# Splitting the row loads' semaphore and fetching the first lone chunk's weights earlier, in a decoder layer on one Trainium2 core

## The reference

```python
x = layernorm(x + mixer(x))            # rmsnorm, causal depthwise conv, min-GRU, GELU feed-forward
x = layernorm(x + cross_attention(x, ctx))   # 16 heads of 64, causal mask
x = layernorm(x + moe(x))
# moe: 16 experts, top 2 of sigmoid(x @ gate_w + gate_b), weights normalised
hg = einsum('bsd,edi->bsei', x, experts_wg); hu = einsum('bsd,edi->bsei', x, experts_wu)
all_outputs = einsum('bsei,eid->bsed', silu(hg) * hu, experts_wd)
return x + shared_mlp(x) + sum(expert_values * selected(all_outputs))
```

## Time and profile before

| | |
|---|---|
| time, median of 3 runs | 1636.52 us (1636.0 to 1638.09) |
| the profiled execution's own time | 1619.51 us |
| its span | 1617.8 us |
| mean granted TensorE clock | 0.938 |
| busy: PE, PEld, DVE, ACT, POOL | 83%, 68%, 59%, 59%, 52% |

### The profile page before, as it was taken

How to read it: one execution, slowest core, us unless ns; L and a number is a source line. 1 busy time by engine, 2 the same in 40 slices (tenths; PEclk the granted TensorE clock), 3 DMA queues, 4 the chain that set the end, 5 groups by cost and what they waited for, 6 DMA issues and landing times. The chain is left out here.

```text
span 1617.8 us, 34460 instructions
## 1 busy us (share of the span) xinstructions
PE 1348.5 (83%) x11280; PEld 1098.5 (68%) x11280; DVE 956.1 (59%) x2616; ACT 946.5 (59%) x3395; POOL 834.8 (52%) x988
## 2 busy tenths in 40 slices
PE   2889897999898988899898998989988998967542
PEld 1667676777786777678776777767776777756442
DVE  3456565565655666566764777556665776555324
ACT  3666656576756666466755667565665766555111
POOL 4343525543555457554556546654566646547244
PEclk9999998999998999889998999989999999989777
DMA  6000000032212312222212212132122212135563
GB/s 207 8 7 8 7 7 15 26 93 59 60 38 83 96 30 67 63 79 78 64 43 69 81 55 71 42 99 79 37 60 82 82 57 61 37 94 154 157 181 84
DMA packets 149425, 109.99 MB, mean 68 GB/s; under 512 B 12736, under 2 KB 144384, under 8 KB 149248
## 3 DMA queue, kind: packets, MB, share of 16 engines
q1 hardware_dynamic: 139328, 89.43, 19.0%
q0 software_dynamic: 8192, 16.79, 3.6%
q10 hardware_dynamic: 1728, 1.57, 0.3%
HBM read 73.14 MB, written 34.60 MB: 67 GB/s over the span
## 5 line engine op out<-in xcount | busy, mean ns | idle before, releaser
L1791 POOL TENSOR_TENSOR pr<-pr,ri 128x480 f32<-128x480 f32 x256 | 251.1, 995 | 303.4 <-DVE ri L1394 299.9
L1068 ACT ACTIVATE pr<-sE,nm 128x120 f32<-128x120 f32 x512 | 178.1, 360 | 240.3 <-DVE nm L1389 222.3
L1056 ACT ACTIVATE pT<-t 120x512 f32<-120x512 f32 x256 | 142.3, 614 | 78.7 <-PE t L528 72.8
L1068 ACT ACTIVATE pr<-sO,nm 128x120 f32<-128x120 f32 x512 | 179.2, 381 | 0.0
L669 PEld LDWEIGHTS sE<-kT,qT 64*128 64x128 f32 x1024 | 131.1, 197 | 55.3 <-issue 55.3
L711 PE MATMUL pvb<-wo,hT 128*128 128x128 f32 x1024 | 137.4, 290 | 31.7 <-DVE hT L1404 31.7
L669 PE MATMUL sO<-kT,qT 64*128 64x120 f32 x1024 | 156.7, 295 | 7.0 <-issue 7.0
L1404 DVE TENSOR_TENSOR hT<-pvb,col 128x512 f32<-128x512 f32 x128 | 87.9, 686 | 126.0 <-PE pvb L702 111.4
L711 PEld LDWEIGHTS pvb<-wo,hT 128*128 128x128 f32 x1024 | 125.8, 200 | 45.5 <-DVE hT L1404 45.0
L669 PE MATMUL sE<-kT,qT 64*128 64x120 f32 x1024 | 155.7, 295 | 0.5 <-issue 0.5
L1820 POOL DMA_INDIRECT sorted_x<-x,slot x128 | 129.8, 1014 | 47.3 <-issue 34.3
(11 more groups left out here) (382 smaller groups left out, 3525.7 us busy)
## 6 DMA issues: line engine op xcount, KB each, us to landing
wq<-in_w_e SPq DMA_DIRECT2D x232, 128.0 KB
sorted_y<-yq SPq DMA_DIRECT2D x68, 256.0 KB
xq<-sorted_x SPq DMA_DIRECT2D x58, 256.0 KB
xt<-in_x SPq DMA_DIRECT2D x16, 256.0 KB, 2.9
sorted_x<-yq SPq DMA_DIRECT2D x16, 256.0 KB, 4.2
cT<-in_ctxT SPq DMA_DIRECT2D x16, 240.0 KB, 3.0
out_y<-y SPq DMA_DIRECT2D x48, 64.0 KB
sorted_x<-x,slot POOLq DMA_INDIRECT x128
```

The lines of the kernel that those rows point to most:

```text
L1056: f(pT[:, 4 * r:4 * r + 4, :], seqs((t0, t1)[r][0:S, :]), ACT.Copy).then_inc(sem[f"probsT{r}_sb"], 1)
L1068: ins = f(pr[:, p % RING, r, i, :], score_banks[r][:, i * S:(i + 1) * S], ACT.Exp, bias=nm[:, p % 2, r, i:i + 1], accum_out=rsum[:, p % 2, ...
L1791: GP.tensor_tensor(pr[:, p % RING, r, :, :], pr[:, p % RING, r, :, :], ri[:, p % 2, r, :, :].to_broadcast([P, 4, S]), ALU.mult).then_inc(s ...
```

## The change

The row loads of chunk 7 signal two semaphores: quads 56 to 59 the first, 60 and 61 the second. One semaphore is given up for it in POOL's prologue. In SP's order the weights of 56 and 57 are loaded in halves of two tiles in slots 4 to 7, and the waits for the buffers move to slot 4. Slot 8 then loads rows 56 to 59 and the weights of 58, in front of its output store; slot 9 the weights of 59; slot 10 those of 60 with a wait for `d_down(54)`. Behind the step only the weights of 61 are left, and `d_store(56)` follows them.

```diff
-ONCE = [..., "mask0", "mask", ..., *[f"xq_last{i}" for i in range(3)], ...]
+ONCE = [..., "mask", ..., *[f"xq_last{i}" for i in range(4)], ...]
 def x_last_in(n):
-    return ("xq_last0", LONE_QUADS) if i < LONE_QUADS else (f"xq_last{1 + (i - LONE_QUADS) // 3}", 3)
+    return ("xq_last0", 4) if i < 4 else ("xq_last1", 2) if i < LONE_QUADS else (f"xq_last{2 + (i - LONE_QUADS) // 3}", 3)
...
-            def w_load(n):
+            def w_load(n, lo=0, hi=QUAD):
...
-                for u in range(QUAD):
+                for u in range(lo, hi):
...
                             d_store(n + s - 3)
+                        if s == 4:
+                            for name in ("a_bank", "ln1_out"):
+                                sp.wait_ge(sem[name], whole(name, G - 1))
+                        if 4 <= s < 8:
+                            w_load(LAST + (s - 4) // 2, s % 2 * 2, s % 2 * 2 + 2)
+                        if s == 8:
+                            for i in range(4):
+                                x_load(LAST + i)
+                        if s == 10:
+                            sp.wait_ge(sem["d_down"], upto("d_down", 0, LAST - 2))
+                        if s >= 8:
+                            w_load(LAST + s - 6)
                         for e, q in sums_in(es, s - 1):
                             e_store(e, q)
-                        if s == 8:
-                            for name in ("a_bank", "ln1_out"):
-                                sp.wait_ge(sem[name], whole(name, G - 1))
-                            for i in range(4):
-                                x_load(LAST + i)
-                        if s >= 8:
-                            w_load(LAST + s - 8)
...
                 x_load(LAST + 4 + i)
-            w_load(LAST + 3)
             sp.wait_ge(sem["d_down"], upto("d_down", 0, LAST - 1))
-            w_load(LAST + 4)
+            w_load(LAST + 5)
             d_store(LAST)
-            w_load(LAST + 5)
             d_store(LAST + 1)
...
-            GP.memset(maskb[:], 0.0).then_inc(sem["mask0"], 1)
+            GP.memset(maskb[:], 0.0).then_inc(sem["ones"], 1)
...
-            pool.wait_ge(sem["mask0"], 1)
+            pool.wait_ge(sem["ones"], 2)
...
-            pool.wait_ge(sem["ones"], 2)
+            pool.wait_ge(sem["ones"], 3)
```

More of the change, by code:

```diff
@@ L123 @@
 LATE_LOADS = ["wk", "wv", "wq", "ff2", "wo", "wrs", "wsd"]
-ONCE = ["waits_held", "mixer_weights", *[f"{n}_in" for n in LATE_LOADS], "w_hi", "w_lo", "ident", "identb", "mask0", "mask", "iota", "iotaf", "ones", "gammas", "bq8", "powers", "pads",
+ONCE = ["waits_held", "mixer_weights", *[f"{n}_in" for n in LATE_LOADS], "w_hi", "w_lo", "ident", "identb", "mask", "iota", "iotaf", "ones", "gammas", "bq8", "powers", "pads",
         "tri", "onesb", "zeros", "xs_zeroed",
-        *[f"xq_last{i}" for i in range(3)], *[f"wq_last{i}" for i in range(4)]]
+        *[f"xq_last{i}" for i in range(4)], *[f"wq_last{i}" for i in range(4)]]
 A_USE = {n: k for k, n in enumerate(
```

## The result

The changed kernel takes 1623.53 us (median of 22 runs, 1612.49 to 1635.32). The kernel before took 1633.23 us in the same comparison (22 runs, 1623.93 to 1638.09). The ratio is 0.9944 with an interval of 0.9925 to 0.9963: a gain of 9.1 us by the ratio, 6.0 to 12.2 by its interval. The forecast was a gain of 14.0 us and a time of 1622.5.

What follows compares the result with a forecast made beforehand. PE was taken as the bound for most of the span, SP's issue order at the chunk's end; 12.2 + 2.4 - 0.6 = 14.0 us off 1636.52 gives 1622.5, range 1620 to 1625, or 1617 to 1628 with rivals (a) and (b).

Steps and rivals of the forecast that it cites:

- the first term: PE's wait for `xq` before the transposes of quad 56 goes, since two semaphores split the row loads: 12.2 us gained.
- The inputs that I named as next: After the hole, attention sum, normalised output and weights of 56 to 58 all come before 1509, at most a tenth late.
- The step that the weights of 58 must come in time: In SP's changed order the weights of 58 land by 1505.4, before `d_up(56)` wants them at 1508.6.
- The second term: Weights two quads ahead remove PE's stall at `d_up(59)` for quad 61's weights: 2.4 us, bounds 1.3 and 2.4.
- rival (a): Only the stall before quad 56 goes; SP loses its lead, quad 61's weights come late again: gain 9 to 12, chance 0.13.
- Expected sign: If the forecast is right, `d_up(59)` runs without a DMA wait, where before it stood 2.44 us.
- The price of the halves: Half a quad in slots 4 to 7 costs SP 2.2 us each, hidden in its idle time; 0.6 us for late landings.
- The sign that I had named as wrong: `d_up(52)` to `d_up(55)` waiting longer for `wq`, or a new wait for `hf` or `keep_sb` at `d_up(56)`.
- rival (c): SP becomes the bound of slots 4 to 7 and stretches each; 3.0 us slower net, time 1639.5, chance 0.03.
- Rival (b), the clock: Without the hole PE's clock stays up, work from 1518.05 to 1522.5 takes 2.6 not 4.4 us: gain 16, chance 0.10.
- move with the quads and do not absorb a gain: PE's later gaps, 7.03 us up to 1546.54 and 7.32 us up to 1570.15, are chained to what goes before them.
- A sign of being right: PE's distance from `d_T(56)` to the last matmul becomes shorter by about 2.4 us.

Runs made afterwards that it cites:

- e6_before_again: The kernel before, without an edit, run again on the second chip for a profile; one execution, 1628.74 us.
- e1_split_only: The kernel before with the two row semaphores alone, SP's order unchanged, first chip; 1552.81 us, ratio 0.9983 to the kernel before.
- e7_registers_early: The changed kernel with eight expert numbers of quads 56 and 57 read into registers in slots 3 and 4; ratios to before 0.9954 (second chip), 0.9941 (third).

## Why the prediction was right, and where it was not

The time came out 1 us from the forecast, but the gain is 9.1 us and not 14.0: the kernel before was timed at 1633.23 us here and 1636.52 when the forecast was made, and this made up most of the shortfall. That nearness is luck. The sign and the first term are not.

**The first term, 12.2 us, was right in place and cause.** The wait for `xq` is gone in all profiles of the change. Between the executions on the second chip it was worth 16.3 us (16.27 against none), so its size varies between executions of before. What varies is SP's lead, the time from the end of `w_load(55)` to the end of `d_down(55)`: 12.8 us in the earlier trace rows and 8.6 in `e6_before_again`. From that end of `w_load(55)` to the transposes there are 25.0 us in the one and 24.9 in the other. The inputs that I named as next were there: `x` came 0.68 us late for the transposes of `x2`, and `d_up(56)` waited for nothing. The step that the weights of 58 must come in time carried more than I gave it: `e1_split_only` shows that without the new order of SP it takes 11.14 of these microseconds back.

**The second term, 2.4 us, failed.** The step was "the sixth quad's weights leave at about 1520.2 ... `d_up(59)` would want them at 1522.3". SP's part of it held: from the end of `w_load(55)` (1506.29) to the end of the sixth quad (1527.41 + 4.72 = 1532.13) it needs 25.8 us, and I had counted 27.1. What failed are the two stretches of PE, both read from one execution. The end of `w_load(55)` came 12.8 us ahead of the end of `d_down(55)` in the earlier trace rows, and 9.6 us ahead in the change (1506.29 against 1515.93). From there to where PE wants `d_up(59)` I had counted 16.4 us (1505.88 to 1522.3), and it took 14.6. So PE reached `d_up(59)` 3.88 us before its weights: 3.2 for the lead, 1.8 for the faster stretch and 0.2 for the landing, less 1.3 that SP was quicker. The lead did not shrink by the halves. `e6_before_again` has none and leads by 8.6 us, the change's three profiles by 9.6, 10.2 and 9.2; on the first chip it is 11.4 without halves, 10.9 with them and 8.4 with them at half the price. Where `d_up(55)` waits for its weights, SP's delay moves PE along. Of the 3.2 us, 1.0 lies between SP's last issue and `d_up(55)`, and 2.2 in PE's way from there to the end of `d_down(55)`, 9.3 us before and 7.2 after. 1.7 of the 2.2 are in one row, here before and after (the granted clock was 0.55 from 1496 to 1506 and 0.77 from 1508.7 to 1516):

```profile
1501.01 3.79 PE L711 MATMUL pvb<-wo,hT 128*128 128x128 f32 x16 [0.80 <-DVE hT L1404]
```

```profile
1512.98 2.05 PE L714 MATMUL pvb<-wo,hT 128*128 128x128 f32 x16 [0.79 <-DVE hT L1407]
```

`e6_before_again` has 2.05 us there too, so this isn't owed to the change: the forecast stood on a slow row of one execution.

This is rival (a) by its outcome (gain 9 to 12; measured 9.1), though not by its reason: SP didn't meet more stalls, PE came earlier. Expected sign: a wait there was to go; it grew by 1.4 us.

**The price of the halves, 0.6 us, was mis-sized.** I had priced late landings, and had called SP's 2.2 us hidden in its idle time. The landings did not move (2.0, 2.1 and 3.0 us at least, middle and most, against the earlier trace rows). SP's time did: it is fully in line in slots 6 and 7 of the first profile, with a half of 2.35 us, an output store of 1.50 instead of 0.35 and a weight quad of 5.09 instead of 3.64. On the first chip this is 6.2 us at the end of `d_down(55)`, by one profile of each kernel. On the others it is up to 5 us by the profiles, and open in the timed runs. The idle time that I had counted as cover was a wait for `d_down`, which ended when PE let it; how long it is depends on where PE stands. The sign that I had named as wrong, `d_up(52)` to `d_up(55)` waiting longer for `wq`, is there at `d_up(54)` and `d_up(55)`. The mechanism is rival (c), below the size from which it turns the sign.

**Rival (b), the clock, was right but small.** The group of transposes took 0.60 us and not 1.12, and from `d_T(56)` to `d_up(57)` there are 5.3 us (1515.76 to 1521.03), where before needed 5.9 (83.0 to 88.9 from the common point). That is 0.6 us, not 2. The work up to the router's first product took 3.8 us and not 4.4; the rival had 2.6 for it, and waits of 0.68 and 0.39 us are most of the rest. By the place where PE wants `d_up(59)` the gain has grown to 1.6 us (14.8 from `d_T(56)`, and 16.4 before), part of it a shorter wait at `d_down(56)`, and the stall there swallows it. The granted clock fell to 0.83 in the window from 1505 to 1515, with PE half busy, and stood at 1.00 behind it. From 1530 to 1550, around the stalls of `d_up(59)` and `d_up(60)`, it is 0.57.

**The tail took some back.** From `d_up(59)` to the transposes of quad 62 there are 33.2 us in the first profile of before and 36.2 in the second; 38.1, 38.2 and 37.3 in the change's three. I had said that these gaps "move with the quads and do not absorb a gain". In these profiles they absorb 1 to 5 us. The wait of `d_up(61)` is not the place by itself: it is 7.2 to 8.7 us in the change, 6.7 and 10.0 before. Behind it, from `d_up(61)` to the transposes, there are 13.0 and 11.9 us before and 16.5, 14.9 and 14.3 in the change, and there `d_down(61)` waits 2.5 to 4.0 us for `gin`, which it didn't before:

```profile
1564.09 2.07 PE L838 MATMUL sO<-wq,gin 128*128 128x128 f32 x8 [4.02 <-DVE gin L1544]
```

What makes it late was not tested. A sign of being right failed with it: from `d_T(56)` to the last matmul PE was to need 2.4 us less than 74.5; it needed 79.1 in the second profile of before and 79.7 to 81.0 in the change.

**The sum on one chip.** Second chip, before to change, in the positions of the quads: the hole 16.4 (16.3, and 0.16 by which the rows of `d_down(55)` and `d_T(56)` overlap in the change), the last slots -4.5 (end of `d_down(55)` at 72.7 and 77.2), `d_T(56)` to `d_up(59)` +0.6 (19.0 and 18.4), the tail -2.1: 10.4 us at the transposes of quad 62 (144.16 and 133.71), and the profiled times differ by 11.8 (1628.74 and 1616.94). The first pair of profiles hid this, because PE took 8.4 us from `d_up(51)` to `d_up(52)` in that execution of before and 14.4 to 15.1 in the other profiles of both kernels on these chips. Weighted over the three comparisons in which the change was timed (0.9944, 0.9968, 0.9898), its ratio is 0.9942.

**A better kernel?** The whole quads in slots 3 and 4 gave 0.9924 and 0.9914 on two chips, 11.8 and 14.1 us below before by these ratios. That is the best pair of ratios here, some 3 us below the change's 0.9942 in the mean. The intervals overlap, and on the third chip the change itself read 0.9898. So it is not shown that it beats the change.

## What to carry to other kernels

A hole that waits on one shared semaphore can have a second input right behind it: list every transfer that the next three instructions need, with the time at which its queue issues it, before you price the first. Idle time of a queue that waits for a buffer is not free time to be filled: where the buffer comes free earlier, each added issue is on the path. When two engines are moved against each other, count both from one point, and read the lead of one over the other from more than one execution: here it was 12.8 us in one profile of the same kernel and 8.6 in the next, and a lead 3 us shorter than the one counted made a stall of 2 us grow instead of go.

## What the runs showed of the hardware

- The same kernel takes 1555.26 us on one chip and 1632.62 and 1634.38 on two others, 5% more. One place where it shows is `d_up(48)` to `d_up(50)`: 15.7 us in all profiles of the first chip, 19.0 to 19.4 in all others.
- On the slower chips DVE stands idle for 3 to 6 us before two to five of the step's `hT`, and the profile names no releaser; PE waits for the result one to three times, 2.0 to 5.0 us each:

```profile
1474.29 0.69 DVE L1407 TENSOR_TENSOR hT<-pvb,col 128x512 f32<-128x512 f32 x1 [5.90 <-remote]
```

  On the first chip no `hT` has such an idle time; DVE waits there for PE. The first profile of before has two (2.90 and 4.79 us), that of `e6_before_again` four, and this is part of why the first looks so fast; `e7_registers_early` has two as well, and is as quick from `d_up(51)` to `d_up(52)` (8.8 us). What DVE waits for is open.
- A weight transfer with its register load costs SP 1.1 to 1.2 us, without it 0.5 to 0.6. The register load is half of the issue time in these runs.
- A stall of 20 to 25 us before `d_up(60)`, with ACT idle and SP's issues slow at once and no releaser named, came in four of the fourteen profiled executions, all of changed kernels on the second or third chip. Its cause is open.
